# Padding each head's columns in the q and k tiles by 16 bytes

## What is computed

```python
h = modulate(layernorm(x), shift_msa, scale_msa)
qkv = (h @ W_qkv + b_qkv).reshape(b, 128, 3, 16, 9)
q, k, v = qkv[:, :, 0], qkv[:, :, 1], qkv[:, :, 2]
scores = einsum('blhd,bmhd->bhlm', q * 9 ** -0.5, k)
o = einsum('bhlm,bmhd->blhd', softmax(scores), v).reshape(b, 128, 144)
x = x + gate_msa * (o @ W_proj + b_proj)
h = modulate(layernorm(x), shift_mlp, scale_mlp)
x = x + gate_mlp * (gelu(h @ W_fc1 + b_fc1) @ W_fc2 + b_fc2)
```

```python
attn = softmax(einsum('nthd,ntkd->nthk', q * scale, k))   # heads t by heads k of one token
out = einsum('nthk,ntkd->nthd', attn, v)
out = out.transpose(0, 2, 1, 3).reshape(n, t, d)
```

## Time and profile before

| | us |
|---|---|
| median of 3 runs | 1681.84 |
| lowest, highest | 1674.70, 1683.79 |
| profiled execution, its own time | 1677.75 |
| its span, first to last instruction | 1676.0 |
| TensorE matmuls busy | 1508.5 (90%) |
| VectorE, ScalarE, GpSimd busy | 934.8, 801.8, 543.7 |
| granted TensorE clock, mean | 0.95 |
| queue q1 (SP's transfers) | 190386 packets, 121.21 MB, 33.3% of the 16 DMA engines |

### The profile page before, as it was taken

One profiled execution on the slowest core, in us unless ns is written; L12 is line 12 of the kernel. 1 busy time (PEld: TensorE's weight loads), 2 busy tenths in 40 slices (PEclk: granted clock), 3 DMA queues, 4 the chain that ended last, 5 costly groups with the idle time before them and its releaser, 6 DMA issues. The chain is left out here.

```text
span 1676.0 us, 41783 instructions
## 1 busy us (share of the span) xinstructions
PE 1508.5 (90%) x16240; PEld 1116.2 (67%) x16240; DVE 934.8 (56%) x2406; ACT 801.8 (48%) x1431; POOL 543.7 (32%) x751
## 2 busy tenths in 40 slices
PE   6659998999999998889899968878799899999998
PEld 4436666777778776666677746666577566666777
DVE  2368885233343322668744778888535466565442
ACT  0236665332333332556655536656545355555543
POOL 0535553111131210344433323434234323432331
PEclk9979999999999999899999968989999889898999
DMA  4455551000011020464501143443224767676021
GB/s 119 135 120 135 130 134 37 8 8 8 8 48 32 22 57 1 105 159 108 115 16 36 52 99 81 102 105 88 64 48 44 109 112 110 107 116 112 16 61 47
DMA packets 209269, 126.25 MB, mean 75 GB/s; under 512 B 143873, under 2 KB 192608, under 8 KB 203890
## 3 DMA queue, kind: packets, MB, share of 16 engines
q1 hardware_dynamic: 190386, 121.21, 33.3%
q10 hardware_dynamic: 18688, 2.36, 1.1%
HBM read 89.56 MB, written 33.18 MB: 73 GB/s over the span
## 5 line engine op out<-in xcount | busy, mean ns | idle before, releaser
L1060 ACT ACTIVATE prob<-banks 128x1024 f32<-128x1024 f32 x256 | 262.0, 1024 | 245.0 <-PE banks L601 244.1
L1325 DVE TENSOR_REDUCE negm<-banks 128x8 bf16<-128x1024 f32 x256 | 311.2, 1216 | 92.4 <-PE banks L579 89.6
L1177 ACT ACTIVATE hid<-banks 128x512 f32<-128x512 f32 x280 | 166.6, 596 | 350.9 <-PE banks L832 350.2
L849 PEld LDWEIGHTS banks<-wfc,hid 128*128 128x128 f32 (+1 forms) x2240 | 284.2, 191 | 11.5 <-issue 9.1
L849 PE MATMUL banks<-wfc,hid 128*128 128x144 f32 (+1 forms) x2240 | 289.3, 287 | 0.2 <-DVE gx L1355 0.2
L831 PE MATMUL banks<-hT,wfc 128*128 128x512 f32 x560 | 288.2, 595 | 0.5 <-ACT hid L1177 0.5
L1648 POOL TENSOR_TENSOR X<-X,gx 128x288 f32<-128x288 f32 x128 | 100.6, 799 | 452.3 <-DVE gx L1355 449.7
L832 PE MATMUL banks<-hr,rfc 66*128 66x512 f32 x280 | 223.6, 799 | 0.0
L579 PE MATMUL banks<-qk 54*128 54x128 bf16 (+1 forms) x2048 | 125.9, 247 | 90.7 <-DVE negm L1325 46.2
L612 PE MATMUL banks<-prob,V 128*32 128x128 f32 x4096 | 174.9, 291 | 2.4 <-ACT OT L1066 2.4
L597 PE MATMUL banks<-qk 54*128 54x128 bf16 (+1 forms) x2048 | 172.4, 240 | 3.7 <-ACT prob L1060 3.7
(11 more groups left out here) (151 smaller groups left out, 2321.9 us busy)
## 6 DMA issues: line engine op xcount, KB each, us to landing
qk<-qk_scr SPq DMA_DIRECT2D x336, 72.0 KB
gbuf<-gate_scr SPq DMA_DIRECT2D x64, 288.0 KB, 4.0
qk_scr<-parts SPq DMA_DIRECT2D x48, 288.0 KB, 2.5
qk<-qk_scr SPq DMA_DIRECT2D x48, 216.0 KB
qk<-tok_scr SPq DMA_DIRECT2D x112, 72.0 KB
qk_scr<-parts SPq DMA_DIRECT2D x48, 144.0 KB, 2.4
qk<-qk_scr SPq DMA_DIRECT2D x48, 144.0 KB
tok_scr<-parts SPq DMA_DIRECT2D x48, 96.0 KB, 4.7
```

The lines of the kernel that those rows point to most:

```text
L849: mm = pe.matmul(bank[4 + q][:, C * (b % 2):C * (b % 2) + C], hid[0:rows, t, T * b:T * b + T], wfc2[0:rows, k, t, :], start=(t == 0), stop ...
L1060: act.activation(prob[:, 2 * (U % 2):2 * (U % 2) + 2, :], pairs[1][:], ACT.Exp, scale=scale).then_inc(a_exp, 1)
L1177: act.activation(hid[0:rows, t, :], bank[2 + i % 2][0:rows, :], func).then_inc(a_gelu, 1)
L1325: dve.tensor_reduce(negm[:, u // 2, :, 4 * (u % 2):4 * (u % 2) + 4], pairs[0][:].rearrange("q s (h k) -> q s h k", k=T), AX.X, ALU.max, ne ...
```

## The change

The head pitch in `qk` grows from 512 to 520 bf16 elements, from 1024 to 1040 bytes; a row of 8 heads from 8192 to 8320. The destination rows of the reads of layers 0 to 2 are then no longer contiguous, and source and destination are written as 8 pieces of 1024 bytes a row. In layer 3 the packets have 1024 bytes as before and only their destinations move. The masks can no longer be written as one flat row, and are written as 48 transfers of 8 rows x 8 x 128 elements in the place of 12 four times as large; the wait is for 48. The 128 columns that layer 3 takes for one operand still lie inside one of a row's 8 blocks of 512. To make room in SBUF, two small tiles, `ss` and `rs`, which hold sums and factors of q's and k's norms in layer 2, go into a part of `wfc2` that is free at that time, beside `rt`, which lies there already. Matmuls, activations and the rest of the program are as they were.

```diff
-        qk = sb("qk", [128, 2, 3, 8, TG], BF16)
+        qk = sb("qk", [128, 2, 3, 8, TG + 8], BF16)
...
-        ss = sb("ss", [T, G, 2 * H])
-        rs = sb("rs", [T, G, 2 * H])
...
-        rt = wfc2[:, E - 1].rearrange("p k c -> p (k c)")[:, TG:TG + G * 2 * H].rearrange("t (b h) -> t b h", b=G)
+        spare = wfc2[:, E - 1].rearrange("p k c -> p (k c)")
+        ss, rs, rt = (spare[:, a:a + G * 2 * H].rearrange("t (b h) -> t b h", b=G) for a in (0, G * 2 * H, TG))
...
             if l < 3:
                 return tile[:, 4 * c + i, T * b:T * b + T]
-            at = (G * c + b) * TG
-            return tile.rearrange("r h t -> r (h t)")[:, at + i:at + TG:4]
+            return tile[:, G * c + b, i:TG:4]
...
                         if l < 3:
-                            q_src, k_src = (qk_scr[p, side, :, :, 8 * s:8 * s + 8].rearrange("a d h t -> (a d) (h t)")
+                            q_src, k_src = (qk_scr[p, side, :, :, 8 * s:8 * s + 8].rearrange("a d h t -> (a d) h t")
                                             for side in range(2))
-                            q_dst = qq[r0:r0 + rows, r].rearrange("r h t -> r (h t)")
-                            k_dst = kk[r0:r0 + rows, r].rearrange("r h t -> r (h t)")
                         else:
                             q_src, k_src = (tok_scr[p, side, 2 * s:2 * s + 2].rearrange("c b a d h w -> (a d) (c b) (h w)")
                                             for side in range(2))
-                            q_dst, k_dst = qq[r0:r0 + rows, r], kk[r0:r0 + rows, r]
+                        q_dst, k_dst = (x[r0:r0 + rows, r, :, 0:TG] for x in (qq, kk))
                         sp.dma_start(q_dst, q_src[0:rows]).then_inc(q_r[r][s], 16)
...
-                            sp.dma_start(qk[row:row + TB, side, r].rearrange("r h t -> r (h t)")
-                                         .rearrange("r (x t) -> r x t", t=T),
-                                         maskb[:, side, :].unsqueeze(1).to_broadcast([TB, 8 * G, T])) \
-                                .then_inc(q_mask, 16)
+                            for x in range(4):
+                                sp.dma_start(qk[row:row + TB, side, r, :, T * x:T * x + T],
+                                             maskb[:, side, :].unsqueeze(1).to_broadcast([TB, 8, T])).then_inc(q_mask, 16)
...
                 if l == 3:
-                    pe.wait_ge(q_mask, 16 * 12)
+                    pe.wait_ge(q_mask, 16 * 48)
```

## The result

| | before | after |
|---|---|---|
| median us | 1681.13 | 1724.87 |
| lowest, highest | 1674.70, 1683.79 | 1711.29, 1734.22 |
| runs | 4 | 4 |
| profiled execution, time and span | 1677.75, 1676.0 | 1728.26, 1726.5 |
| granted clock, mean | 0.950 | 0.935 |

The ratio is 1.0239 with a 95% interval of 1.0195 to 1.0283: the change makes the kernel 2.4% slower, 44 us. The forecast was 1679 us in a range of 1665 to 1706.

The account below looks back on a forecast made before the run. It took TensorE's work plus its waits as the bound. Reads 0.4 us shorter at waits in layers 0 to 2 gave 3.4 us, everything else nothing; moved to the median and rounded up, 1679 us, range 1665 to 1706.

Parts of the forecast that it names:

- The packets' size: Reads of layers 0 to 2: eight 1024-byte packets take 568 ns against 565 for one of 8192, the same rate.
- The starts: Destinations in `qk` off the old boundaries: up to +3.0 us a group, nothing in the sum, +1.5 inside the range.
- The slower rival: Each packet starting off the old boundaries makes an additional small piece: +1.5 us a group, 1706 us; chance 0.21.
- The slower rival's sum of waits: TensorE's waits for reads: 13.5 us at nine waits, 6 in layer 3, 5 at ten near waits; 24.5 us.
- The ten groups with 1 us of room 0.5 each: Ten groups of layers 0 to 2 that start without a wait would lose 0.5 us each, 5 us.
- The masks: SP in layer 2: 48 issues at 0.34 to 0.37 us take 16 to 18 us, against 15.99 for twelve; no cost.
- The cover of 9 us behind the gate: Gates of layer 2's second MLP group leave 9 us before DVE's use, so 5 us more of masks costs nothing.
- The nine engines: Reads into `qk`: 55% of 16 engines is nine working without a break; few engines and destination rows are the limit.
- The rival in which small packets share a destination better: Reads of layers 0 to 2: eight smaller packets interleave, reads 2 us shorter, 13.6 us gained, 1668 us; chance 0.17.

Follow-up runs that it names:

- the run from the copy in HBM: Kernel before with 48 mask transfers, their source a copy of the masks in HBM instead of the SBUF tile; 1692.83 us in one execution.
- the one with later masks: Changed kernel with its 48 mask transfers issued 16 behind each of three gate loads; 1717.68 us, ratio to before 1.0205.
- the turn: Kernel before with each group's 18 reads issued alternately for the two halves of the heads, not nine and nine; 1652.22 us, ratio 0.9839.

## Why the prediction was wrong

**The packets' size: right for the time, not for the rate.** The prediction took the rate from layer 3, 568 against 565 ns, and so no cost for small packets. Small packets alone gave 1.0009. But the same group with small packets shows 598 ns for a row and not 568, and 501 for 470 with reads in turn: the rate is not the same, only the landing is. The rule of fixed cost per packet (the Trainium skill, "DMA: Bandwidth & Descriptors", section "Bandwidth") would have meant 8%, an estimate. The trace has some 6% of it in the engines' time and none in the kernel's.

**The starts: the step that failed.** The prediction saw that no row of before had such a start, bounded it by +3.0 us a group and then wrote "I take nothing for it in the sum", since other delays would cover it. Measured by the distance it is 18.9 - 17.7 = +1.2 us in layers 0 to 2 and 19.5 - 17.3 = +2.2 in layer 3; by the landing, over all groups, +1.0 and +1.5. All lie inside the bound; the distance in layer 3 is outside the half of it that the range took. The cover doesn't exist: the price is there with the crowding and without it. The slower rival had the mechanism, the sign and, per group, nearly the size; the prediction gave it 0.21 and the sum nothing.

The prediction also counted the starts wrongly. It has "seven of eight" off the boundaries, at offsets of 0 to 112; as told above it is fifteen of sixteen, at up to 240. The Trainium skill, "DMA: Bandwidth & Descriptors", section "How a descriptor splits into AXI transactions", was cited for it with an estimate of +0.9 us a group. By the same count the sixteen starts add 64 beats to 512, twice the share, so the estimate should have been some +1.9 us. The runs agree that starts off 256 bytes cost. They don't follow the Trainium skill's count of beats: by that a packet 16 bytes past the boundary costs one beat more and one 128 bytes past four (an estimate), while the runs have 16 as dearer than 128.

**What a longer read is worth.** The slower rival's sum of waits, 24.5 us, is near the 26.4 that the profile has, in part by luck. "The ten groups with 1 us of room 0.5 each" is right: five of these ten now wait (14 waits for 9), 5.9 us for its 5. The nine that waited before grew by 8.3 us where it had 13.5, and layer 3 by 12.2 where it had 6. What no term of it holds is that attention lost more than its waits, 29.7 us. The windows view of attention 3, before and after, shows the rest:

```profile
1335.14:1580.40 245.26, 229.19 (x3116) 164.43 (x3115) 147.79 (x299) 131.18 (x220) 85.72 (x114) 0.92 0.61 101
```

```profile
1370.80:1630.90 260.10, 231.49 (x3115) 166.36 (x3114) 147.72 (x298) 131.22 (x220) 85.82 (x114) 0.90 0.62 95
```

TensorE stands 12.5 us longer in it and is busy 2.3 us longer with the same matmuls, at a granted clock of 0.90 for 0.92. Two of the four waits of layer 3 are now over 8 us where the longest was 3.3, far more than the price of a start. A late group that makes the next one's parts late would do that, but no run shows it, and among the kernels with unmoved starts one had such a wait too (7.2 us, with small packets). I had added the waits one by one.

**The masks: a second step that failed.** "48 at the 0.34 to 0.37 us of a read's issue" took the price of a transfer from HBM for one inside SBUF. An issue took 0.69 us, and 0.31 only in the run from the copy in HBM. Rows 9 had issues with both ends in SBUF all along, at 1.33 us for four times the packets. The cover of 9 us behind the gate was right and was named, but the masks became 20 us longer and not the 5 that it allows for. The price was 7.9 us in MLP 2 with the masks alone (121.4 for 113.5) and 9.2 between the changed kernel and the one with later masks (124.3 for 115.1), and +0.66% of the time in the run with the masks alone.

**The nine engines: wrong.** The prediction put the limit down to "how few engines, and how few destination rows, take part": the turn bears out that something other than the count of engines holds the reads, and its likeliest reading is the second half. For the first half nothing speaks: q's reads cut for more engines were slower, with four more issues beside them. The rival in which small packets share a destination better fell as well.

The sum of the parts: masks +0.66%, starts with small packets between +1.73 and +3.30% by place, small packets 0.09%. The changed kernel's 2.39% less its masks, 2.05 by the run with later masks, lies in that span. No run moves the statistics (`ss`, `rs`) alone; the span was measured in kernels that leave them where they were, so nothing is left over that would need them. I don't claim the rest, some microseconds that the clock in MLP 0 and 1 gives or takes in single executions.

## What to carry to other kernels

Before padding a tile to break up a transfer, look where each piece then starts: pad by a multiple of 256 bytes (which no run here tried) or leave it. A pitch that is a little off drifts: look at the starts of all rows, not of the first. Count transfers with both ends in SBUF by their own issue time, and look at what the queue holds behind them. When reads are the wait, try the order of their issue first: transfers in turn to far rows were worth 1.6% here, at no memory.

## What the runs showed of the hardware

- Packets of 1024 bytes took 87 ns each in the changed kernel and 75 at unmoved destinations (group 8); reads whose packets all start 16 to 128 bytes past landed 0.8 to 1.8 us a group later in layers 0 to 2 (18.3 to 19.3 for 17.5). One start off the boundary in packets of 8192 bytes cost nothing to be seen (17.5 for 17.4). That starts off 256 bytes cost agrees with the Trainium skill, "DMA: Bandwidth & Descriptors", section "How a descriptor splits into AXI transactions"; the order of 16 and 128 bytes does not.
- Eight packets of 1024 bytes took 598 ns of an engine for 565 of one of 8192 (501 for 470 with reads in turn), and the reads landed as early.
- An issue on SP took 0.31 us from HBM to SBUF, 0.32 from SBUF to HBM, and 0.69 from SBUF to SBUF (medians), for 64 packets of 256 bytes in the first and the last.
- The 1.77 MB of a group landed 17.4 us after the first issue when nine transfers to rows 0 to 53 went ahead of nine to rows 64 to 117, and 14.1 us after it when the two took turns (means of layers 0 to 2).
- The granted clock of a full stretch of TensorE (368 us of MLP without a wait) was 1.00 in some executions and 0.98 in others, worth 6 us.
